# Weighted values as 64x64 squares of the array, interleaved with the scores, with no copies of the values

## The chip, the cores and the metric

The kernel runs on one core of one Trainium2 chip. The metric is the device time of one execution in microseconds (us); lower is better. Three runs of the kernel before took 3058.30, 3062.69 and 3063.12 us.

## What is computed

The input is 8 sequences of 1024 tokens with 128 features. The network is a sandwich: half of a two-layer local-attention block, then a global attention, then half of the same local block again.

```python
x = x + 0.5 * ffn(layernorm(x))      # two layers of local attention + gated MLP
x = x + attn(layernorm(x))           # one global attention, 1024 x 1024 per sequence
x = x + 0.5 * ffn(layernorm(x))      # the same two layers again
```

The change lies in the local attention (8 heads of 64 features, windows of 64 tokens). Of each layer this part matters:

```python
q, k, v = split(shift_token(x) @ wqkv)             # 512 columns each
q, k = rotary(l2norm(q) * q_scale), rotary(l2norm(k) * k_scale)
# window w of 64 queries sees the keys of windows w-1 and w (w = 0: its own only)
sim = q_w @ concat(k_{w-1}, k_w).T                 # 64 x 128 for each head
sim = where((i < j) | (i > j + 64), -inf, sim)     # i: query, j: key
o_w = softmax(sim) @ concat(v_{w-1}, v_w)          # 64 x 64 for each head
x = x + o @ wo
```

## The kernel before, in words

Everything is float32, apart from the mask, which is bf16. The 8192 tokens are 64 tiles of 128 tokens (8 tiles make a sequence; `m` is the tile's place in it, 0 to 7; `row` its place among the 64; `n` counts tiles over all layers). There are `LAYERS` = 4 local layers, so 256 tiles are worked on in all. A tile holds two windows: its queries 0 to 63 see keys 64 to 127 of the tile before and its own keys 0 to 63; its queries 64 to 127 see its own 128 keys.

Each engine has its own program, written out by hand as functions that are called slot by slot; semaphores tie them together. `program` runs, for each layer, `local_slot(L, s)` for s = 0 to 65, then `mlp_slot` for the 15 remaining groups of the MLP; the global attention runs between layers 1 and 2. Slot s of a local layer is a software pipeline: TensorE works on the scores of tile s, the weighted values of tile s - 1, the output projection of tile s - 2, the projections of tiles s + 3 and s + 4 and the transposes of q and k of tile s + 2. The order on TensorE in an ordinary slot (s from 1 to 59) is:

1. `scores(s)`: 4 bf16 matmuls write the mask into banks 3 and 4 of PSUM (L1184), then 16 float32 matmuls in 64x64 squares of the array add q @ k.T on top (L1194 for queries 0 to 63, L1196 for queries 64 to 127). Head 2*hh + i uses array rows 64*i to 64*i + 63 and bank 3 + i; the window of queries picks the array's columns. A float32 matmul appears in the profile as two passes, so there are 16 + 16 passes of L1194 and L1196 for a tile.
2. `weigh_values(s - 1)`: 16 matmuls with 128 rows (all keys of a window) and 64 columns (the queries), 65 elements long (64 features and a column of ones that gives the softmax's sum); L1238 for queries 64 to 127 from `v`, L1241 for queries 0 to 63 from `vprev`. Heads 0 to 3 go to bank 7, heads 4 to 7 to bank 2. Two passes each: 16 + 16.
3. `heads_transpose(s - 2)` (L1226), the q or k projection (L1264), the v projection (L1285), the other q or k projection (L1264), `project_out(s - 2)` (L1296), `weights_transpose(s, 0)` and `(s, 1)` (L1316), `keys_transpose` (L1330), `queries_transpose` (L1346).

In the last slots of a layer (s from 60 to 63, the branch `NT - 4 <= s < NT`) no q and k are projected any more, and `weights_transpose(s, 0)` comes right after `heads_transpose` and at most a v projection.

`vprev` is a second copy of the values, turned by half a tile, so that the 128 keys of the first window lie on partitions 0 to 127: SyncE's queue makes it with two DMAs for each tile (L437, L439), after waiting for ScalarE's copy of v (L594). `weigh_values` waits for them, and so does ScalarE before it writes v's next tile but two.

The other engines: VectorE takes the maxima of the scores (L789, both halves wait for `scores_ready`, which the last scores matmul raises), the reciprocal of the sums (L797, waits for `pv_ready`), the division (L804), the rotary products (L775, L780), sums of squares (L835) and the scaled q and k (L813). ScalarE takes the exponents (L566, after the maxima), squares (L573), and the copies out of PSUM: v (L594), oT (L587), probsT (L600), kT (L609, L610), qT (L612). In an ordinary slot ScalarE copies oT before the exponents; in the last slots it takes exponents 0 first. GpSimd takes the root (L491) and the sum q*cos + q*sin (L496); in layers 0 and 2 it also normalises two tiles in every second slot (L508 to L516). In each layer slot 64 (s == NT) has only the weighted values of the last tile.

The keys of a tile lie in `kT[rows, m % 4, head pair, 0:192]`: before, columns 0 to 63 hold the last 64 keys of the tile before and columns 64 to 191 the tile's own.

Of the kernel before, what the change touches and what calls it, by code (L numbers as in the profile page):

```python
# [13 lines left out]
P = 128  # L14
# [13 lines left out]
KT = WIN + P  # L28
VU = P + 3
# [22 lines left out]
def window_masks():  # L52

    i = np.arange(P)[:, None] % WIN
    j = np.arange(P)[None, :]
    open_ = (j >= i) & (j <= i + WIN)
    first = open_ & (j >= WIN)
    return np.stack([np.tile(np.where(m, 0.0, MASKED), (1, 4)) for m in (first, open_)]).astype(np.float32)  # L60
# [32 lines left out]
def before(t, k, times=1):  # L93


    return times * (t.n + 1 - k)
# [14 lines left out]
def macaron(nc, x_in, wq_in, bq_in, wk_in, bk_in, wv_att_in, bv_in, wo_att_in, bo_in,  # L111
# [15 lines left out]
    with ExitStack() as ctx:  # L127
# [10 lines left out]
        def bank(i, lo=0, hi=BANK, rows=slice(0, P)):  # L138
# [16 lines left out]
        mask = sb("mask", [P, 2, BANK], BF16)  # L155
# [13 lines left out]
        v = sb("v", [P, 4, HEADS, HD1])  # L169
        vprev = sb("vprev", [P, 4, HEADS, HD1])  # L170
# [22 lines left out]
        mask32 = probs.rearrange("p (t c) -> p t c", t=2)  # L193
# [12 lines left out]
        early = vprev[:].rearrange("p a b c -> p (a b c)")  # L206
# [18 lines left out]
         pv_ready, rsum_ready, o_ready, oT_psum, oT_ready, attn_ready, x1_ready,  # L225
# [6 lines left out]
         pv_ready rsum_ready o_ready oT_psum oT_ready attn_ready x1_ready stats_ready  # L232
# [9 lines left out]
        vprev_ready = [sem(f"vprev_ready{i}") for i in range(4)]  # L242
# [6 lines left out]
        def tile_at(L, row):  # L249
            return Tile(L, row, L * NT + row, row % MT) if 0 <= row < NT else None  # L250
# [87 lines left out]
        def _(sp):  # L338
# [91 lines left out]
            def local_slot(L, s):  # L430
                if t := late_tile(L, s + 6):
                    store_blocks(t)
                if t := late_tile(L, s + 5):
                    load_blocks(t)
                if t := tile_at(L, s + 3):
                    wait(sp, v_ready, before(t, 0))
                    sp.dma_start(vprev[WIN:P, t.m % 4], v[0:WIN, t.m % 4]).then_inc(vprev_ready[t.m % 4], 16)  # L437
                    lo = v[WIN:P, (t.m - 1) % 4] if t.m else v[0:WIN, 0]
                    sp.dma_start(vprev[0:WIN, t.m % 4], lo).then_inc(vprev_ready[t.m % 4], 16)  # L439
                if s == 2:  # L440
                    load_output(L)
                if s in (NT - 16, NT - 12, NT - 8):
                    load_tokens(L, (s - NT + 16) // 4)
# [115 lines left out]
        def _(act):  # L559
# [547 lines left out]
        def _(pe):  # L1107
# [62 lines left out]
            def scores(t):  # L1170

                wait(pe, qT_ready, before(t, 0))
                wait(pe, kT_ready, before(t, 0, 2))
                wait(pe, x1_ready, before(t, 3))
                wait(pe, probs_ready, before(t, 1, 2))
                if t.row == 0 and t.L == DEPTH:
                    pe.wait_ge(theta_ready, NT)
                    pe.wait_ge(pT_ready, 2 * NT)
                elif t.row == 0:
                    wait(pe, hid_ready, 3 * NG * t.L)  # L1180
                for w in range(2):
                    for i in range(2):
                        rows, queries = slice(WIN * i, WIN * i + WIN), slice(WIN * w, WIN * w + WIN)
                        nc.tensor.matmul(bank(3 + i, rows=queries), windows16[rows, queries],  # L1184
                                         mask[rows, 0 if w == 0 and t.m == 0 else 1, :],
                                         start=True, stop=False, skip_group_check=True)
# [42 lines left out]
            def weigh_values(t):  # L1229

                pe.wait_ge(vprev_ready[t.m % 4], 32 * (t.n // 4 + 1))
                wait(pe, o_ready, before(t, 1, 2))
                pe.wait_ge(probsT_ready, 2 * t.n + 2)
                for h in range(HEADS):
                    at_h = (h % 2) * BANK + (h // 2) * P
                    col = (h % 4) * HD1
                    bk = (7, 2)[h // 4]
                    nc.tensor.matmul(bank(bk, col, col + HD1, slice(WIN, P)),  # L1238
                                     probsT[:, at_h + WIN:at_h + P], v[:, t.m % 4, h, :],
                                     start=True, stop=True)  # L1240
                    last = nc.tensor.matmul(bank(bk, col, col + HD1, slice(0, WIN)),  # L1241
                                            probsT[:, at_h:at_h + WIN], vprev[:, t.m % 4, h, :],
                                            start=True, stop=True)
                last.then_inc(pv_ready, 1)
# [105 lines left out]
            def local_slot(L, s):  # L1350
# [11 lines left out]
                elif s == 0:  # L1362
# [6 lines left out]
                    scores(tile(0))  # L1369
# [7 lines left out]
                elif NT - 4 <= s < NT:  # L1377
                    scores(tile(0))
                    weigh_values(tile(-1))
# [13 lines left out]
                elif s < NT:  # L1393
                    scores(tile(0))
                    weigh_values(tile(-1))
# [15 lines left out]
                elif s == NT:  # L1411
                    weigh_values(tile(-1))
# [157 lines left out]
```

## Time and profile before

| | us |
|---|---|
| three runs: lowest, median, highest | 3058.30, 3062.69, 3063.12 |
| the profiled execution: its own time | 3062.09 |
| its span in the profile | 3060.3 |
| busy: TensorE (PE) | 2986.1 |
| busy: VectorE (DVE) | 2588.4 |
| busy: ScalarE (ACT) | 2093.9 |
| busy: GpSimd (POOL) | 1748.7 |

How to read it: the durations of matmuls are modelled and neighbouring matmuls overlap, so the busy time of TensorE says that it is hardly ever without work, and not how fast it goes. How fast it goes is read from the distance between the starts of its instructions. PEld is the loading of TensorE's weights, which overlaps the matmuls; its operand is the one that is kept in the array.

### The profile page before, as it was taken

How to read it: one execution, taken by the hardware profiler on the slowest of the kernel's cores; microseconds unless marked ns; L12 is line 12 of the kernel's file. 1: busy time of each engine (PE TensorE's matmuls, PEld its weight loads, DVE VectorE, ACT ScalarE, POOL GpSimd, SP SyncE). 2: the span in 40 equal slices, each digit the busy share in tenths (PEclk: the TensorE clock that was granted, in tenths of full speed). 3: DMA queues.
4: the chain of work that ended last, by engine and by line, in shares of the span. 5: the costliest groups of instructions: out<-in, count | busy, mean ns of one | idle time of the engine just before them, and what ended most of it. 6: DMA issues, size and time to landing. Idle time of an engine off the chain costs nothing.

```text
span 3060.3 us, 84552 instructions
## 1 busy us (share of the span) xinstructions
PE 2986.1 (98%) x30773; PEld 2157.1 (70%) x30773; DVE 2588.4 (85%) x5526; ACT 2093.9 (68%) x5016; POOL 1748.7 (57%) x1158
## 2 busy tenths in 40 slices
PE   7999999999999999989999799999999999999999
PEld 4777777667777777656777577777766677777765
DVE  7999998668888888858999699999866788888866
ACT  4777777436777777328889477777753677777742
POOL 8888886125666665541000688888721566666610
PEclk9999999999999999999999899999999999999999
DMA  5222222102222232100000122222320122222221
GB/s 131 50 50 52 51 57 63 45 18 48 51 49 52 50 64 60 41 1 1 1 1 1 24 52 52 51 51 56 65 52 14 43 50 52 50 52 58 57 49 42
DMA packets 311515, 138.26 MB, mean 45 GB/s; under 512 B 225897, under 2 KB 276546, under 8 KB 311106
## 3 DMA queue, kind: packets, MB, share of 16 engines
q1 hardware_dynamic: 311106, 132.84, 19.9%
q8 instruction: 252, 4.13, 0.6%
q14 instruction: 157, 1.29, 0.1%
HBM read 28.13 MB, written 19.66 MB: 16 GB/s over the span
## 4 chain that ended last, share of the span: by engine, by line
PE 90%; DVE 4%; issue 2%; POOL 2%; ACT 1%; SPq 0%; DMA 0%; DVEq 0%; ACTq 0%; POOLq 0%
PE psum L1264 14%; PE psum L1139 11%; PE psum L1238 8%; PE psum L1285 7%; PE psum L1296 7%; PE psum L1316 7%; PE psum L1194 6%; PE psum L1165 5%; PE psum L1226 5%; PE psum L1330 3%; PE psum L1346 3%; PE psum L1529 3%; PE psum L1505 3%; PE psum L1184 3%; PE psum L1515 2%
## 5 line engine op out<-in xcount | busy, mean ns | idle before, releaser
L491 POOL TENSOR_TENSOR rnorm<-ssq_floor,neg_half 128x16 f32<-128x16 f32 x256 | 750.7, 2932 | 491.0 <-DVE qkr L813 486.2
L566 ACT ACTIVATE shared<-psum,neg_max 128x128 f32<-128x128 f32 x2048 | 596.6, 397 | 39.8 <-DVE neg_max L789 39.8
L496 POOL TENSOR_TENSOR qk_cos<-qk_cos,qk_sin 128x1024 f32<-128x1024 f32 x256 | 607.3, 2372 | 0.0
L1264 PE MATMUL psum<-wqkv,hT 128*128 128x512 f32 x1024 | 532.2, 603 | 17.7 <-DVE qk_sin L775 9.5
L587 ACT COPY shared<-psum 128x512 f32<-128x512 f32 x256 | 150.3, 587 | 435.0 <-PE psum L1226 435.0
L775 DVE TENSOR_TENSOR qk_sin<-psum,sin 128x512 f32<-128x512 f32 x512 | 350.5, 685 | 97.9 <-ACT sq L573 96.6
L780 DVE TENSOR_TENSOR qk_cos<-psum,cos 128x512 f32<-128x512 f32 x512 | 350.6, 685 | 78.6 <-ACT sq L573 78.4
L625 ACT ACTIVATE shared<-psum,b1g 128x512 f32<-128x512 f32 (+1 forms) x192 | 131.7, 686 | 355.2 <-PE psum L1139 352.0
L1139 PE MATMUL psum<-shared,w1g 128*128 128x512 f32 (+1 forms) x768 | 347.2, 595 | 5.4 <-DVE shared L879 4.0
L573 ACT ACTIVATE sq<-psum 128x512 f32<-128x512 f32 x512 | 334.6, 654 | 25.2 <-PE psum L1264 25.2
L1296 PEld LDWEIGHTS psum<-wo,shared 128*128 128x128 f32 x2048 | 267.5, 191 | 115.7 <-issue 115.0
L789 DVE TENSOR_REDUCE neg_max<-psum 128x4 f32<-128x512 f32 x512 | 321.2, 666 | 23.6 <-PE psum L1196 23.4
L835 DVE TENSOR_REDUCE ssq<-sq 128x16 f32<-128x1024 f32 x256 | 309.4, 1209 | 0.6 <-POOL ssq_floor L488 0.6
L813 DVE TENSOR_TENSOR qkr<-qk_cos,rnorm 128x1024 f32<-128x1024 f32 x256 | 303.8, 1187 | 6.9 <-issue 6.3
L1238 PE MATMUL psum<-v,shared 128*64 128x65 f32 x4096 | 293.6, 224 | 0.0
L1241 PE MATMUL psum<-vprev,shared 128*64 128x65 f32 x4096 | 293.4, 224 | 0.0
L1238 PEld LDWEIGHTS psum<-v,shared 128*64 128x64 f32 x4096 | 258.1, 137 | 46.4 <-issue 46.4
L600 ACT COPY shared<-psum 128x512 f32<-128x512 f32 x512 | 285.3, 621 | 5.9 <-PE psum L1316 5.9
L1264 PEld LDWEIGHTS psum<-wqkv,hT 128*128 128x128 f32 x1024 | 177.3, 193 | 150.6 <-issue 139.3
L1285 PE MATMUL psum<-wqkv,hT 128*128 128x512 f32 x512 | 281.5, 632 | 0.0
L1316 PE MATMUL psum<-ident,shared 128*128 128x128 f32 x2048 | 270.7, 273 | 8.8 <-ACT shared L566 4.0
L1296 PE MATMUL psum<-wo,shared 128*128 128x128 f32 x2048 | 270.9, 275 | 0.0
(132 smaller groups left out, 6382.5 us busy)
## 6 DMA issues: line engine op xcount, KB each, us to landing
vprev<-v SPq DMA_DIRECT2D x512, 130.0 KB, 2.3
token_blocks<-blocks SPq DMA_DIRECT2D x236, 64.0 KB, 1.6
hT<-token_blocks SPq DMA_DIRECT2D x944, 16.0 KB, 1.8
shared<-Y SPq DMA_DIRECT2D x32, 256.0 KB
shared<-Y SPq DMA_DIRECT2D x32, 224.0 KB
out<-X SPq DMA_DIRECT2D x8, 512.0 KB, 3.2
X<-in_L_attn_x SPq DMA_DIRECT2D x7, 512.0 KB, 6.5
wqkv<-in_L_ffn_wqkv SPq DMA_DIRECT2D x4, 512.0 KB, 3.9
```

What stands on the lines that cost most here:

```text
L491: nc.gpsimd.tensor_tensor(rnorm[:], ssq_floor[:], neg_half[:], ALU.pow).then_inc(rnorm_ready, 1)
L496: nc.gpsimd.tensor_tensor(both, both, qk_sin[:, t.m % 2, :], ALU.add).then_inc(sum_ready, 1)
L566: last = nc.scalar.activation(probs[:, c * P:(c + 1) * P], bank(3 + i, (c % 4) * P, (c % 4 + 1) * P), ACT.Exp, bias=neg_max[:, c:c + 1])
L573: nc.scalar.activation(sq[:, i * INNER:(i + 1) * INNER], bank(i), ACT.Square).then_inc(sq_ready, 1)
L775: nc.vector.tensor_tensor(y, x[:, :, ::-1, :], part.unsqueeze(1).to_broadcast([P, HEADS, 2, DH // 2]), ALU.mult).then_inc(rot_ready, 1)
L780: nc.vector.tensor_tensor(heads(qk_cos[:, t.m % 2, i * INNER:(i + 1) * INNER]), heads(bank(i)), cos[:, t.m, i:i + 1, :].to_broadcast([P, H ...
L1139: last = nc.tensor.matmul(bank(banks[half], rows=slice(0, size)), w1g[:, half * HID + lo:half * HID + lo + size], zT, start=True, stop=True)
L1238: nc.tensor.matmul(bank(bk, col, col + HD1, slice(WIN, P)), probsT[:, at_h + WIN:at_h + P], v[:, t.m % 4, h, :], start=True, stop=True)
L1264: nc.tensor.matmul(bank(i), hT[:, t.m * P:(t.m + 1) * P], wqkv[:, i * INNER:(i + 1) * INNER], start=True, stop=True).then_inc(qk_psum, 1)
L1285: nc.tensor.matmul(bank(v_bank(t)), hT[:, t.m * P:(t.m + 1) * P], wqkv[:, 2 * INNER:3 * INNER], start=True, stop=True).then_inc(v_psum, 1)
L1296: last = nc.tensor.matmul(bank(out_bank(t), 0, P), oT[:, c * P:(c + 1) * P], wo[:, c, :], start=(c == 0), stop=(c == INNER // P - 1))
L1316: last = nc.tensor.transpose(bank(6 + i, (c % 4) * P, (c % 4 + 1) * P), probs[:, c * P:(c + 1) * P], ident[:])
```

## The change

The weighted values are computed in 64x64 squares, like the scores: for each head and window of queries, the own and the other 64 keys are two matmuls that add up in PSUM. Each has 64 rows, 64 columns and 65 elements, so a tile has 32 matmuls (64 passes) in place of 16 (32 passes); a first tile of a sequence (m = 0) has 28. They are made in two parts. In part 0 the array's upper rows work on heads 0 to 3 (bank 7) and its lower rows on heads 4 to 7 (bank 2); in part 1 it is the other way round and the sums are completed. Part 1 waits for a new semaphore, `pv_begun`, that part 0's last matmul raises. The scores are cut in two halves too (head pairs 0 and 1, then 2 and 3), and the order is scores half 0 (with the mask), values part 0, scores half 1, values part 1. In slot 0 the two halves of the scores follow each other, in slot 64 the two parts of the values do.

The keys of the tile now lie first in `kT` (columns 0 to 127), and those of the tile before in columns 128 to 191, so that a window's own keys have the same partitions in `probsT` as in `v`. For queries 0 to 63 the scores' moving operand is two pieces of 64 columns, 128 apart. The mask has three variants (768 KB in float32 instead of 512 KB), turned to fit.

`vprev`, its 512 DMAs, its semaphores and all waits for them are gone; `v` has five buffers instead of four, and the weights of the global attention, which lay in `vprev`'s space, have a tensor `early` of their own.

```diff
@@ sync: local_slot
-                if t := tile_at(L, s + 3):
-                    wait(sp, v_ready, before(t, 0))
-                    sp.dma_start(vprev[WIN:P, t.m % 4], v[0:WIN, t.m % 4]).then_inc(vprev_ready[t.m % 4], 16)
-                    lo = v[WIN:P, (t.m - 1) % 4] if t.m else v[0:WIN, 0]
-                    sp.dma_start(vprev[0:WIN, t.m % 4], lo).then_inc(vprev_ready[t.m % 4], 16)
@@ scalar: values, rotated
-                if u := tile_at(t.L, t.row - 3):
-                    act.wait_ge(vprev_ready[u.m % 4], 32 * (u.n // 4 + 1))
-                nc.scalar.copy(v[:, t.m % 4, :, 0:DH], heads(bank(v_bank(t)))).then_inc(v_ready, 1)
+                nc.scalar.copy(v[:, t.n % VALUES_KEPT, :, 0:DH], heads(bank(v_bank(t)))).then_inc(v_ready, 1)
...
-                nc.scalar.copy(kT[:, (t.m + 1) % 4, :, 0:WIN], src[:, :, WIN:P]).then_inc(kT_ready, 1)
-                nc.scalar.copy(kT[:, t.m % 4, :, WIN:KT], src).then_inc(kT_ready, 1)
+                nc.scalar.copy(kT[:, (t.m + 1) % 4, :, P:KT], src[:, :, WIN:P]).then_inc(kT_ready, 1)
+                nc.scalar.copy(kT[:, t.m % 4, :, 0:P], src).then_inc(kT_ready, 1)
@@ tensor: scores(t, second): waits and mask only if not second
-                lo = 0 if t.m else WIN
-                for hh in range(4):
+                blocks_of = 2 if t.m else 1
+                for hh in (2, 3) if second else (0, 1):
                     for i in range(2):
                         rows = slice(DH * i, DH * i + DH)
                         q = qT[rows, t.m % 2, hh, :]
                         k = kT[rows, t.m % 4, hh, :]
-                        nc.tensor.matmul(bank(3 + i, hh * P + lo, (hh + 1) * P, slice(0, WIN)), q[:, 0:WIN],
-                                         k[:, lo:P], start=False, stop=True, skip_group_check=True)
+                        own_then_before = k.rearrange("p (b j) -> p b j", j=WIN)[:, 0:2 * blocks_of - 1:2, :]
+                        to = bank(3 + i, hh * P, hh * P + blocks_of * WIN, slice(0, WIN)).rearrange("p (b j) -> p b j", j=WIN)
+                        nc.tensor.matmul(to, q[:, 0:WIN], own_then_before, start=False, stop=True, skip_group_check=True)
                         last = nc.tensor.matmul(bank(3 + i, hh * P, (hh + 1) * P, slice(WIN, P)), q[:, WIN:P],
-                                                k[:, WIN:KT], start=False, stop=True, skip_group_check=True)
-                last.then_inc(scores_ready, 1)
+                                                k[:, 0:P], start=False, stop=True, skip_group_check=True)
+                if second:
+                    last.then_inc(scores_ready, 1)
@@ tensor: weigh_values
-                pe.wait_ge(vprev_ready[t.m % 4], 32 * (t.n // 4 + 1))
-                wait(pe, o_ready, before(t, 1, 2))
-                pe.wait_ge(probsT_ready, 2 * t.n + 2)
-                for h in range(HEADS):
-                    at_h = (h % 2) * BANK + (h // 2) * P
-                    col = (h % 4) * HD1
-                    bk = (7, 2)[h // 4]
-                    nc.tensor.matmul(bank(bk, col, col + HD1, slice(WIN, P)),
-                                     probsT[:, at_h + WIN:at_h + P], v[:, t.m % 4, h, :], start=True, stop=True)
-                    last = nc.tensor.matmul(bank(bk, col, col + HD1, slice(0, WIN)),
-                                            probsT[:, at_h:at_h + WIN], vprev[:, t.m % 4, h, :], start=True, stop=True)
-                last.then_inc(pv_ready, 1)
+                if second:
+                    pe.wait_ge(pv_begun, t.n + 1)
+                else:
+                    wait(pe, v_ready, before(t, 0))
+                    wait(pe, o_ready, before(t, 1, 2))
+                    pe.wait_ge(probsT_ready, 2 * t.n + 2)
+                for j in range(HEADS // 2):
+                    for i in range(2):
+                        h = j + HEADS // 2 * (second ^ i)
+                        at_h = (h % 2) * BANK + (h // 2) * P
+                        col = (h % 4) * HD1
+                        rows = slice(WIN * i, WIN * i + WIN)
+                        for w in range(2):
+                            alone = w == 0 and t.m == 0
+                            if alone and i == 1:
+                                continue
+                            n = t.n - 1 if i > w else t.n
+                            last = nc.tensor.matmul(bank((7, 2)[h // 4], col, col + HD1, slice(WIN * w, WIN * w + WIN)),
+                                                    probsT[rows, at_h + WIN * w:at_h + WIN * w + WIN],
+                                                    v[rows, n % VALUES_KEPT, h, :], start=j == 0 and (alone or not second),
+                                                    stop=alone or bool(second), skip_group_check=True)
+                last.then_inc(pv_ready if second else pv_begun, 1)
@@ tensor: local_slot, both branches from s = 1 to NT - 1
-                    scores(tile(0))
-                    weigh_values(tile(-1))
+                    for second in range(2):
+                        scores(tile(0), second)
+                        weigh_values(tile(-1), second)
```

## Rows read from the trace of the kernel before

**Rows 1.** The page: busy time, granted clock in 40 slices, chain that ended last.
```profile
PE 2986.1 (98%) x30773; PEld 2157.1 (70%) x30773; DVE 2588.4 (85%) x5526; ACT 2093.9 (68%) x5016; POOL 1748.7 (57%) x1158
...
PEclk9999999999999999999999899999999999999999
...
PE 90%; DVE 4%; issue 2%; POOL 2%; ACT 1%; SPq 0%; DMA 0%; DVEq 0%; ACTq 0%; POOLq 0%
```

**Rows 2.** PE timeline, an ordinary slot: start us, length us, line, count.
```profile
311.93 0.41 PE L1184 MATMUL psum<-mask,windows 64*64 64x512 bf16 x4
312.17 0.27 PE L1194 MATMUL psum<-kT,qT 64*64 64x128 f32 x2
312.17 0.27 PE L1196 MATMUL psum<-kT,qT 64*64 64x128 f32 x2
312.27 0.27 PE L1194 MATMUL psum<-kT,qT 64*64 64x128 f32 x2
...
312.94 0.27 PE L1196 MATMUL psum<-kT,qT 64*64 64x128 f32 x2
313.14 0.27 PE L1238 MATMUL psum<-v,shared 128*64 128x65 f32 x1
...
313.25 0.22 PE L1238 MATMUL psum<-v,shared 128*64 128x65 f32 x1
...
314.07 0.22 PE L1238 MATMUL psum<-v,shared 128*64 128x65 f32 x1
...
314.22 0.66 PE L1226 MATMUL psum<-ident,shared 128*128 128x128 f32 x4
...
320.11 0.41 PE L1184 MATMUL psum<-mask,windows 64*64 64x512 bf16 x4
```

**Rows 3.** PE timeline, a sequence's first tile: its L1194 has 64 columns.
```profile
303.99 0.22 PE L1194 MATMUL psum<-kT,qT 64*64 64x64 f32 x2
303.99 0.27 PE L1196 MATMUL psum<-kT,qT 64*64 64x128 f32 x2
304.04 0.28 PE L1194 MATMUL psum<-kT,qT 64*64 64x64 f32 x3
```

**Rows 4.** PEld timeline: weight loads right after PE had waited.
```profile
41.62 0.13 PEld L1184 LDWEIGHTS psum<-mask,windows 64*64 64x64 bf16 x4 [1.50 <-issue]
41.65 0.20 PEld L1194 LDWEIGHTS psum<-kT,qT 64*64 64x64 f32 x2
```

**Rows 5.** ACT timeline, the slots of rows 2: copies of oT and probsT.
```profile
314.92 0.59 ACT L587 COPY shared<-psum 128x512 f32<-128x512 f32 x1 [1.84 <-PE psum L1226]
...
318.90 1.11 ACT L600 COPY shared<-psum 128x512 f32<-128x512 f32 x2
```

**Rows 6.** DVE timeline, the slot that begins at 320.11.
```profile
321.64 1.25 DVE L789 TENSOR_REDUCE neg_max<-psum 128x4 f32<-128x512 f32 x2
...
325.25 0.69 DVE L775 TENSOR_TENSOR qk_sin<-psum,sin 128x512 f32<-128x512 f32 x1 [0.43 <-ACT sq L573]
```

**Rows 7.** POOL timeline, a sum and the next tile's root.
```profile
312.58 2.37 POOL L496 TENSOR_TENSOR qk_cos<-qk_cos,qk_sin 128x1024 f32<-128x1024 f32 x1
...
316.72 2.93 POOL L491 TENSOR_TENSOR rnorm<-ssq_floor,neg_half 128x16 f32<-128x16 f32 x1 [1.55 <-DVE qkr L813]
```

**Rows 8.** Timelines of DVE, ACT and PE in slot 61 of layer 0.
```profile
540.53 1.29 DVE L789 TENSOR_REDUCE neg_max<-psum 128x4 f32<-128x512 f32 x2 [2.27 <-PE psum L1196]
...
541.26 1.14 ACT L566 ACTIVATE shared<-psum,neg_max 128x128 f32<-128x128 f32 x4 [1.01 <-DVE neg_max L789]
...
542.45 0.66 PE L1316 MATMUL psum<-ident,shared 128*128 128x128 f32 x4 [0.33 <-ACT shared L566]
```

**Rows 9.** DVE timeline, an early slot of layer 2.
```profile
1757.12 1.23 DVE L813 TENSOR_TENSOR qkr<-qk_cos,rnorm 128x1024 f32<-128x1024 f32 x1 [0.95 <-issue]
```

**Rows 10.** DMA issues of the whole span: count, KB each, us to landing.
```profile
vprev<-v SPq DMA_DIRECT2D x512, 130.0 KB, 2.3
```

**Rows 11.** The tile `mask`: ns min/median/max, when, form.
```profile
L948 DVE CAST mask<-shared x1: 683/683/683, 29.2 to 29.2; 128x1024 bf16<-128x1024 f32 x1
```

More of the change, by code:

```diff
@@ L59, in window_masks @@
     first = open_ & (j >= WIN)
-    return np.stack([np.tile(np.where(m, 0.0, MASKED), (1, 4)) for m in (first, open_)]).astype(np.float32)
+    turned = [np.roll(m, WIN, axis=1) for m in (first, open_)]
+    return np.stack([np.tile(np.where(m, 0.0, MASKED), (1, 4)) for m in turned + [open_]]).astype(np.float32)
 class Tile:
@@ L154, in macaron @@
         sin = sb("sin", [P, MT, 2, DH])
-        mask = sb("mask", [P, 2, BANK], BF16)
+        mask = sb("mask", [P, 3, BANK], BF16)
         windows16 = sb("windows16", [P, P], BF16)
@@ L168, in macaron @@
         kT = sb("kT", [P, 4, 4, KT])
-        v = sb("v", [P, 4, HEADS, HD1])
-        vprev = sb("vprev", [P, 4, HEADS, HD1])
+        v = sb("v", [P, VALUES_KEPT, HEADS, HD1])
+        early = sb("early", [P, 10 * P + 3])
         neg_max = sb("neg_max", [P, HEADS])
@@ L1168, in combine, with scores @@
                 last.then_inc(mlp_ready, 1)
[L1170 to L1186, printed above, removed]
-                lo = 0 if t.m else WIN
-                for hh in range(4):
+            def scores(t, second):
+                if not second:
+                    wait(pe, qT_ready, before(t, 0))
+                    wait(pe, kT_ready, before(t, 0, 2))
+                    wait(pe, x1_ready, before(t, 3))
+                    wait(pe, probs_ready, before(t, 1, 2))
+                    if t.row == 0 and t.L == DEPTH:
+                        pe.wait_ge(theta_ready, NT)
+                        pe.wait_ge(pT_ready, 2 * NT)
+                    elif t.row == 0:
+                        wait(pe, hid_ready, 3 * NG * t.L)
+                    for w in range(2):
+                        for i in range(2):
+                            rows, queries = slice(WIN * i, WIN * i + WIN), slice(WIN * w, WIN * w + WIN)
+                            nc.tensor.matmul(bank(3 + i, rows=queries), windows16[rows, queries],
+                                             mask[rows, 2 if w else 1 if t.m else 0, :],
+                                             start=True, stop=False, skip_group_check=True)
+                blocks_of = 2 if t.m else 1
+                for hh in (2, 3) if second else (0, 1):
                     for i in range(2):
@@ L1227, in heads_transpose, with weigh_values @@
                 last.then_inc(oT_psum, 1)
-            def weigh_values(t):
-                pe.wait_ge(vprev_ready[t.m % 4], 32 * (t.n // 4 + 1))
-                wait(pe, o_ready, before(t, 1, 2))
-                pe.wait_ge(probsT_ready, 2 * t.n + 2)
-                for h in range(HEADS):
-                    at_h = (h % 2) * BANK + (h // 2) * P
-                    col = (h % 4) * HD1
-                    bk = (7, 2)[h // 4]
-                    nc.tensor.matmul(bank(bk, col, col + HD1, slice(WIN, P)),
-                                     probsT[:, at_h + WIN:at_h + P], v[:, t.m % 4, h, :],
-                                     start=True, stop=True)
-                    last = nc.tensor.matmul(bank(bk, col, col + HD1, slice(0, WIN)),
-                                            probsT[:, at_h:at_h + WIN], vprev[:, t.m % 4, h, :],
-                                            start=True, stop=True)
-                last.then_inc(pv_ready, 1)
+            def weigh_values(t, second):
+                if second:
[5 more added lines that the diff above has]
+                for j in range(HEADS // 2):
+                    for i in range(2):
+                        h = j + HEADS // 2 * (second ^ i)
+                        at_h = (h % 2) * BANK + (h // 2) * P
+                        col = (h % 4) * HD1
+                        rows = slice(WIN * i, WIN * i + WIN)
+                        for w in range(2):
+                            alone = w == 0 and t.m == 0
[7 more added lines that the diff above has]
+                last.then_inc(pv_ready if second else pv_begun, 1)
             def project_qk(t, i):
@@ L1368, in local_slot @@
                         pe.wait_ge(consts_done, 9)
-                    scores(tile(0))
+                    scores(tile(0), 0)
+                    scores(tile(0), 1)
                     project_v(tile(3))
@@ L1393, in local_slot @@
                 elif s < NT:
-                    scores(tile(0))
-                    weigh_values(tile(-1))
+                    for second in range(2):
+                        scores(tile(0), second)
+                        weigh_values(tile(-1), second)
                     if t := tile(-2):
@@ L1411, in local_slot @@
                 elif s == NT:
-                    weigh_values(tile(-1))
+                    weigh_values(tile(-1), 0)
+                    weigh_values(tile(-1), 1)
                     heads_transpose(tile(-2))
```

10 lines of the change are left out of this document (4 added, 6 removed).

## The prediction, made before the change was run

> **What bounds the kernel.** I read the page first. TensorE is busy 98% of the span and carries 90% of the chain that ended last [rows 1]. The reader is to see that only what changes the distance between TensorE's starts changes the time, as long as VectorE (85%), the next engine, keeps up. So the second view is TensorE's timeline over an ordinary slot [rows 2]. Masks of two tiles that follow each other start at 311.93 and 320.11, so a slot takes 8.18 us, and this distance repeats unchanged from slot 4 to slot 59 of every layer. In such a slot TensorE waits for nobody. The third views are the timelines of ScalarE, VectorE and GpSimd in the same slots [rows 5 to 7], for the slack that each leaves, and of a layer's last slots [rows 8], where TensorE does wait.
>
> **The passes themselves: no gain.** A tile's values take 32 passes in two column halves of the array. L1238 starts at 313.14, 313.25 and for the sixteenth time at 314.07 [rows 2]: after the first distance of 0.11 the other 14 take 0.82, so 0.058 us each for 65 elements. Afterwards there are 64 passes in four squares, again 16 rounds. If four squares go side by side, a round costs what it costs now. For that, scores are the nearest rows: two L1194 and two L1196 start at 312.17 within the resolution of the row, the next L1194 at 312.27, and 8 rounds of four go from 312.17 to 312.94, 0.11 us each [rows 2]. A square whose scores have only 64 columns takes its next pass after 0.05 to 0.06 us (303.99 to 304.04) while the other two squares work [rows 3]. So both halves of the claim are seen, four at once and 0.058 for such a short pass, but not together. The dearest end is that passes can't follow faster than they do in scores, 0.11 / 4 = 0.027 us each: 64 x 0.027 = 1.74 us where the values' 0.93 us (313.14 to 314.07) and their two seams are now. The cheapest end is that nothing changes: 16 x 0.058 = 0.93. I take this end, as rows 3 stand nearer to it (two squares at 0.058 and two at 0.11 are 0.019 per pass, already beyond 0.027).
>
> **The seam between scores and values: the gain.** Scores use 64x64 squares, the values 128x64. From the last round of scores (312.94) to the first pass of values are 0.20 us where a round of scores takes 0.11, and from there to the second pass 0.11 where a pass takes 0.058 [rows 2]. Without a change of shape the two distances should be 0.11 and 0.058: the seam costs 0.31 - 0.17 = 0.14 us. It goes. The change from the values to the 128-row transposes (314.07 to 314.22) remains, as does the one ahead of the mask, so nothing else is saved. The new order has three seams, all within one shape. The trace has one of this kind, mask to scores: 0.24 us (311.93 to 312.17 [rows 2]) for 512 bf16 columns, which at TensorE's full clock of 2.4 GHz, granted nearly throughout [rows 1], are 0.21. So a seam costs between nothing and 0.03 us. I take nothing, because in this one the operands change from bf16 to float32 too, and keep 0.03 for one seam of each slot (8 us) for the range.
>
> By the Trainium skill (TensorEngine Tiling (Array Packing), Key Properties) a change of tiling mode drains TensorE, and a change of tile alone doesn't. The 0.14 us at the seam agree [rows 2]; how much is drain and how much the first load, the rows don't tell.
>
> **Ordinary slots.** 8.18 - 0.14 = 8.04 us. They are 56 in each layer (4 to 59), 224 in all. Slots 1 to 3 of layers 1 and 3 show no wait that binds either: 6 more. 230 x 0.14 = 32.2 us saved. In slots 1 to 3 of layers 0 and 2 GpSimd's sum is late (VectorE stands 0.95 us before L813 [rows 9]) and TensorE waits behind it; there I count no gain.
>
> Does another engine stop 8.04 us? The moved step is the second half of the scores: `scores_ready` now comes 8 rounds of 0.058, 0.47 us, after where it did. Behind it stand VectorE's maxima, and behind them on its queue the sums, L813, L804 and L775. Counted from the mask at 320.11, the last scores end at 320.11 + 1.01 + 0.27 = 321.39 and would end at 321.86; VectorE starts the maxima at 321.64, so they come 0.2 us later, and in this slot VectorE has 0.43 us idle before L775 [rows 6], which takes it up. In the slot before, VectorE is busy with statistics until after the new time. GpSimd's loop in layers 0 and 2: the root waits for L813, and over two slots this is the tightest loop. The sum ends at 314.95 and the root starts at 316.72, with L813's 1.18 us between [rows 7]; the remaining 0.59, less some 0.2 for passing on, leaves 0.4 of slack over two slots, and 0.28 are taken from them. It fits, narrowly. ScalarE has 1.84 us idle before L587 [rows 5].
>
> The new order wants probsT earlier: the values start 0.24 + 4 x 0.11 = 0.68 after the mask, not 1.21. ScalarE's copy ends at 318.90 + 1.11 = 320.01 [rows 5], the values would start at 320.79. Fulfilled.
>
> **The new wait, `pv_begun`.** Part 1 waits until part 0's last matmul is done; queued behind it on TensorE is all else. Let T be the start of part 0's last pass. It is done at T + 0.22; passing on costs 0.04 (L1226 ends at 314.88, L587 starts at 314.92 [rows 2, 5]) and taking up 0.05 (L566 ends at 542.40, L1316 starts at 542.45 [rows 8]): T + 0.31. Scores half 1 fills T + 0.06 to T + 0.49. So its cover has 0.18 us to spare. After a wait, six loads start within 0.03 us, four of the mask and two of the scores [rows 4], so the queue fills quickly. Where the cover is missing, in slot 64, the wait costs 0.31 - 0.06 = 0.25: 4 layers, 1.0 us. If the cover failed wholly in the other slots, they would lose 0.25 instead of nothing.
>
> **The last slots: a loss.** In slots 61 to 63 the chain is scores, maxima (starts 540.53 right after L1196), exponents (541.26), and TensorE waits 0.33 us for these with L1316 [rows 8]. With `scores_ready` 0.47 later, each of these slots becomes 0.47 longer instead of 0.14 shorter. In slot 60 TensorE doesn't wait yet, but by the same chain would now by some 0.2, less 0.14: 0.05. Sum 3 x 0.47 + 0.05 = 1.45, in 4 layers 5.8 us.
>
> **DMAs and the rest.** 512 DMAs of 130 KB go, 2.3 us each to landing [rows 10]. No wait of TensorE ends on one, and SyncE's queue loses two waits ahead of the token blocks, which aren't late: nothing gained, at the cheapest end 1 us from slots in which tokens come early. The mask's load grows by half and its cast from 0.68 to 1.0 us [rows 11]; it stands in VectorE's queue at the start, where TensorE waits for VectorE: 0.5 us, at most 1.3 with the longer transfer. ScalarE's copies have the same sizes. The scores' moving operand in two pieces costs nothing or at most the difference of two 64-column passes to one of 128, 2 x 0.058 - 0.11 = 0.007 in 8 rounds, 0.06 us a tile, 14 us in all; I take nothing, since nothing is read twice.
>
> **Sum.** -32.2 + 5.8 + 1.0 + 0.5 = -24.9 us. The profiled execution took 3062.1 us (its span 3060.3); 3037.2. The median of the runs is 0.6 above it: 3038 us. A change by less than 0.2% (6 us) can't be told from none here.
>
> **Rivals.** *A, the squares don't keep the pace (slower).* Place: the passes of `weigh_values`. It decides from (0.93 + 0.14) / 64 = 0.0167 us per pass on; four squares at the round of 0.058 are 0.0145, the fastest the trace shows is 0.019 [rows 3]. At 0.019 a tile loses 0.15 net, over 256 tiles +38, and 3108 us with the last slots; at 0.027 a tile loses 0.67 net, +172 and some 3240. Against it: six loads within 0.03 us [rows 4], and four scores passes that start together [rows 2]. Chance 0.15.
>
> The Trainium skill (TensorE: Matmul & The Clock Gate, Wait — 56ns, not 53.3ns?) states that start-to-start never falls below about 25 ns for a small matmul; this is nearly the case of 0.027 above. Estimated from that page, 64 x 25 ns = 1.6 us, +0.53 a tile, some 3205 us. This case's trace disagrees for different squares (four passes start together) and leaves the average open.
>
> *B, the wait shows.* Completion of a pass in a square may be told later than I take. Each 0.1 us of lateness beyond 0.18 costs 0.1 a slot; at 0.1 exposed (0.28 late) the gain of 25 is gone, with 0.25 exposed the time is 3095. Chance 0.07.
>
> *C, another engine takes over.* VectorE with GpSimd in layers 0 and 2, or the last slots lose more: half of the ordinary gain, 3038 + 16 = 3054. For it: 0.4 of slack against 0.28. Chance 0.08.
>
> Forecast: 0.70, with its own range of 3024 (passes at 0.056, 8 us; slots 1 to 3 of layers 0 and 2 gain too, 1 us; the last slots lose nothing, 5.8) to 3052 (the operand in two pieces or the seams and half of the former). B below 0.1 exposed and C still are faster. Range of 8 in 10: 3022 to 3075, which takes in C and the milder half of B, and leaves out A (0.15). Faster 0.77, same 0.07 (B near its deciding point, the edge of C), slower 0.16.
>
> **What would show it.** Masks in ordinary slots 8.04 apart; the first pass of values 0.11 after the last scores round of half 0, with four squares each 0.058; no stand of TensorE ahead of part 1 except in slot 64; L1316 of the last slots waiting about 0.8 instead of 0.33; no L1330 wait for VectorE in ordinary slots. Wrong would make it: rounds of values over 0.067 us, a gap of over 0.1 after scores half 1, or VectorE's L813 standing for GpSimd in every second slot.

## The result

The changed kernel takes 3045.61 us (median of 4 runs, 3039.54 to 3046.97), the kernel before 3062.52 us (4 runs, 3058.3 to 3063.12). The ratio is 0.9944, its 95% interval 0.9931 to 0.9958: 0.56% faster, 17 us where 25 were forecast. The profiled execution has a span of 3044.0 us, 16.3 less than before.

First the page of the changed kernel: TensorE's busy time and passes, and the DMA queues (packets, MB, share of 16 engines).

```profile
PE 2956.9 (97%) x38453; PEld 2167.1 (71%) x38453; DVE 2601.1 (85%) x5526; ACT 2090.6 (69%) x5016; POOL 1751.8 (58%) x1158
...
q1 hardware_dynamic: 270274, 64.91, 9.8%
q8 instruction: 312, 5.11, 0.7%
```

TensorE has 7680 passes more (38453 against 30773 [rows 1]): 256 x 32 more for the values, less 512 that the first tiles of the sequences leave out. (Such a tile has 24 matmuls of values, not 28 as the section on the change says.) For the doubled passes of the values the time went down, so squares do overlap. The instruction queue moves 312 packets of 16 KB; it moved 252 before: 60 more for 2 x 7680 = 15360 more instructions of TensorE (a load and a matmul for each pass), so one packet for each 256.

Next TensorE's timeline of the changed kernel in an ordinary slot (start us, length us, line, count), the counterpart of [rows 2].

```profile
317.62 0.41 PE L1178 MATMUL psum<-mask,windows 64*64 64x512 bf16 x4
317.86 0.27 PE L1190 MATMUL psum<-kT,qT 64*64 64x128 f32 x2
...
318.19 0.27 PE L1191 MATMUL psum<-kT,qT 64*64 64x128 f32 x2
318.30 0.64 PE L1244 MATMUL psum<-v,shared 64*64 64x65 f32 x32
318.76 0.27 PE L1190 MATMUL psum<-kT,qT 64*64 64x128 f32 x2
...
319.09 0.27 PE L1190 MATMUL psum<-kT,qT 64*64 64x128 f32 x2
...
319.20 0.64 PE L1244 MATMUL psum<-v,shared 64*64 64x65 f32 x32
319.77 0.44 PE L1222 MATMUL psum<-ident,shared 128*128 128x128 f32 x2
```

The first values start 0.11 after the last round of scores (318.19 to 318.30): the 0.20 of before is gone. The 32 passes of part 0 take 318.30 to 318.76, 8 rounds of 0.0575. Scores half 1 follows without a gap, and so does part 1 at 319.20. Next the view by stages, over the whole slot: its length, busy us of PE, PEld, DVE, ACT and POOL with the number of instructions, granted clock, DMA share, GB/s.

```profile
317.62:325.65 8.03, 8.03 (x135) 6.12 (x135) 7.37 (x15) 6.33 (x18) 7.59 (x7) 1.00 0.09 18
```

8.03 us where 8.18 were. That is the slot of the prediction, 8.04. But not all ordinary slots look so. Reading the starts of the masks (L1178) through the trace, 199 of the 224 ordinary slots take 8.03 us within 0.03 and the other 25 take 0.15 to 1.07 more, 9.4 us in all; before, no ordinary slot differed from 8.18. This is slot 4 of layer 0, again TensorE's timeline.

```profile
74.87 0.41 PE L1178 MATMUL psum<-mask,windows 64*64 64x512 bf16 x4
...
76.45 0.63 PE L1244 MATMUL psum<-v,shared 64*64 64x65 f32 x26
77.81 0.34 PE L1244 MATMUL psum<-v,shared 64*64 64x65 f32 x6 [0.74 <-issue]
...
83.97 0.41 PE L1178 MATMUL psum<-mask,windows 64*64 64x512 bf16 x4
```

The slot takes 9.10 us. After 26 of the 32 passes of part 1 TensorE stands, and the cause is "issue": no semaphore that the profile knows. Of the 25 stands 20 are inside the values, 4 right behind them (ahead of L1222) and one behind the transposes that follow (ahead of L1268). This was in no step of the prediction.

The last slots of a layer, the counterpart of [rows 8]: TensorE and VectorE in slot 61 of layer 0, and then TensorE's rows of the same slot before that [rows 8] doesn't have.

```profile
533.57 0.41 PE L1178 MATMUL psum<-mask,windows 64*64 64x512 bf16 x4
535.71 0.66 PE L1222 MATMUL psum<-ident,shared 128*128 128x128 f32 x4
537.32 0.66 PE L1320 MATMUL psum<-ident,shared 128*128 128x128 f32 x4 [0.95 <-ACT shared L561]
537.81 1.14 PE L1300 MATMUL psum<-wo,shared 128*128 128x128 f32 x8
538.83 0.66 PE L1320 MATMUL psum<-ident,shared 128*128 128x128 f32 x4
...
540.29 0.41 PE L1178 MATMUL psum<-mask,windows 64*64 64x512 bf16 x4
```
```profile
535.39 1.29 DVE L782 TENSOR_REDUCE neg_max<-psum 128x4 f32<-128x512 f32 x2 [2.84 <-PE psum L1191]
```
```profile
539.17 0.41 PE L1184 MATMUL psum<-mask,windows 64*64 64x512 bf16 x4
...
541.47 0.66 PE L1226 MATMUL psum<-ident,shared 128*128 128x128 f32 x4
542.45 0.66 PE L1316 MATMUL psum<-ident,shared 128*128 128x128 f32 x4 [0.33 <-ACT shared L566]
542.94 1.14 PE L1296 MATMUL psum<-wo,shared 128*128 128x128 f32 x8
544.24 0.63 PE L1316 MATMUL psum<-ident,shared 128*128 128x128 f32 x4
```

Slot 61 takes 6.72 us instead of 6.50. TensorE waits 0.95 us for the exponents instead of 0.33, since the maxima start 1.82 us after the mask (535.39 less 533.57) instead of 1.36 (540.53 less 539.17). L1320 starts 3.75 us after the mask, where L1316 started 3.28 after it: 0.47 later, as forecast. Its second group starts only 0.19 later (5.26 instead of 5.07), because before TensorE also lost time between L1296 and that group (1.30 us from start to start, now 1.02). So the slot grows by 0.22 and not by 0.47.

So the account of the span, from the masks' starts in the two traces, is:

| stretch | forecast | measured |
|---|---|---|
| ordinary slots, 224 x (8.18 to 8.03) | -31.4 | -33.6 |
| stands inside the values | 0 | +9.4 |
| slots 0 to 3 of the four layers | -0.8 | +0.5 |
| slots 60 to 62, four layers | +4.0 | +3.3 |
| slots 63 and 64 and what follows | +2.9 | +3.9 |
| before the first mask | +0.5 | +0.3 |
| sum (of the unrounded terms) | -24.9 | -16.2 |

One trace is not the median of the runs. The fifth row holds the stretch from slot 63 of layer 1 over the global attention, which takes 518.4 to 525.2 us in the nine traces; in this trace it is 1.5 us longer than before, in the second trace of the same kernel (below) 0.9 shorter. The other three layers lose 0.79 us each in both. In that second trace the sum is -18.0, with stands of 9.5 us.

### The profile page after: what moved, and what is told of

It reads as the page before. It is cut to its first block, busy times and chain, and to the rows that moved or that the text cites. A ratio compares the mean times of both kernels' runs of the same rounds, so it can differ in the third digit from the quotient of the medians.

```text
span 3044.0 us, 99399 instructions
## 1 busy us (share of the span) xinstructions
PE 2956.9 (97%) x38453; PEld 2167.1 (71%) x38453; DVE 2601.1 (85%) x5526; ACT 2090.6 (69%) x5016; POOL 1751.8 (58%) x1158
## 4 chain that ended last, share of the span: by engine, by line
PE 91%; DVE 3%; POOL 2%; issue 2%; ACT 1%; SPq 0%; DMA 0%; DVEq 0%; ACTq 0%; POOLq 0%
PE psum L1268 14%; PE psum L1132 11%; PE psum L1244 8%; PE psum L1300 7%; PE psum L1289 7%; PE psum L1320 7%; PE psum L1190 6%; PE psum L1158 5%; PE psum L1222 5%; PE psum L1334 4%; PE psum L1350 3%; PE psum L1537 3%; PE psum L1513 3%; PE psum L1178 3%; PE psum L1523 2%
## 5 line engine op out<-in xcount | busy, mean ns | idle before, releaser
L1268 PE MATMUL psum<-wqkv,hT 128*128 128x512 f32 x1024 | 534.5, 606 | 19.2 <-DVE qk_sin L768 10.3
L782 DVE TENSOR_REDUCE neg_max<-psum 128x4 f32<-128x512 f32 x512 | 328.0, 682 | 73.9 <-PE psum L1191 73.8
L1244 PE MATMUL psum<-v,shared 64*64 64x65 f32 x15872 | 342.1, 218 | 3.7 <-issue 3.0
L1244 PEld LDWEIGHTS psum<-v,shared 64*64 64x64 f32 x15872 | 317.9, 134 | 9.1 <-issue 7.5
L1191 PE MATMUL psum<-kT,qT 64*64 64x128 f32 x4096 | 308.0, 270 | 0.0
L1190 PE MATMUL psum<-kT,qT 64*64 64x128 f32 (+1 forms) x4096 | 301.3, 264 | 0.0
L1268 PEld LDWEIGHTS psum<-wqkv,hT 128*128 128x128 f32 x1024 | 178.2, 194 | 153.5 <-issue 141.7
L1320 PE MATMUL psum<-ident,shared 128*128 128x128 f32 x2048 | 271.5, 274 | 14.8 <-ACT shared L561 11.6
```

The source lines that it names most:

```text
L1190: nc.tensor.matmul(to, q[:, 0:WIN], own_then_before, start=False, stop=True, skip_group_check=True)
L1244: last = nc.tensor.matmul(bank((7, 2)[h // 4], col, col + HD1, slice(WIN * w, WIN * w + WIN)), probsT[rows, at_h + WIN * w:at_h + WIN * w ...
L1268: nc.tensor.matmul(bank(i), hT[:, t.m * P:(t.m + 1) * P], wqkv[:, i * INNER:(i + 1) * INNER], start=True, stop=True).then_inc(qk_psum, 1)
L1320: last = nc.tensor.transpose(bank(6 + i, (c % 4) * P, (c % 4 + 1) * P), probs[:, c * P:(c + 1) * P], ident[:])
```

## The experiments

All runs below are measured against the kernel before on their chip, 3062.2 to 3062.7 us. Theory F: the stands come where TensorE's queue runs dry because a block of its instructions is fetched too late for the dense stretch of squares. Theory T: they come from something that runs beside the kernel in time.

**The changed kernel again.**

> The changed kernel once more, for the comparison on one chip and for a second trace. In its first trace TensorE stands without a wait (cause 'issue') inside part 1 of the values in some 20 of the 224 ordinary slots, by 0.2 to 1.07 us, 9.4 us in all; in layer 0 in slots 4, 5, 18, 31, 32 and 46. Theory F (these stands are TensorE's queue running dry where a block of its instructions has to be fetched, so their place goes with the count of instructions): the same slots of layer 0 again, within one; 3037 to 3049 us. Theory T (they come from something that runs in time beside the kernel): other slots.

3046.91 us (5 runs, 3044.11 to 3049.79), ratio 0.9951 (0.9938 to 0.9963). In its trace the stands of layer 0 are in slots 4, 5, 18, 19, 31, 32 and 46, and 9.5 us in all: the same places within one slot, with other lengths. In the other layers the places come back too, apart from slot 42 of layer 2 (0.56 us in the first trace).

**128 instructions ahead of everything.**

```diff
@@ tensor: ahead of program
             pe.wait_ge(consts_done, 4)
+            for _ in range(32):
+                nc.tensor.matmul(bank(7, 0, 1), ident[:], ident[:, 0:1], start=True, stop=True)
             program(local_slot, mlp_slot, global_slot)
```

> The changed kernel with 32 one-column matmuls (128 instructions of TensorE: 64 passes with their weight loads) ahead of everything, into a bank that nobody reads; it adds work that the reference doesn't need. A slot has 278 instructions of TensorE, 246 where the values are those of a sequence's first tile, 274 on average, 18 more than 256. Theory F with blocks of 256 instructions (the instruction queue moves packets of 16 KB): 128 instructions more put the stands of layer 0 some 128 / 18 = 7 slots away from 4, 5, 18, 31, 32, 46, so near 11, 25, 38 or 39, 53. Theory T: no such shift; the same slots, or any.

3049.6 us (one run), 9.9 us of stands. Its first mask starts at 50.53 us instead of 41.91, behind the added matmuls, so its time isn't to be compared with the others. In layer 0 they are now in slots 11, 12, 24, 38, 40, 53 and 54, where theory F put 11, 25, 38 or 39, and 53. Slots 4, 5, 18, 31, 32 and 46 take 8.03 us. This is slot 24 of layer 0, on TensorE's timeline; two passes of part 1 come late.

```profile
244.29 0.41 PE L1178 MATMUL psum<-mask,windows 64*64 64x512 bf16 x4
...
245.79 0.70 PE L1244 MATMUL psum<-v,shared 64*64 64x65 f32 x28
...
247.18 0.27 PE L1244 MATMUL psum<-v,shared 64*64 64x65 f32 x2 [0.68 <-issue]
```

So a stand belongs to a place in the sequence of TensorE's instructions, with a period of 256 of them. Theory T has fallen.

The traces allow a closer look, as they hold each packet of the instruction queue with its start and duration, and every instruction of TensorE, semaphore instructions included. Counted from the first of these as 0, all 25 stands of the changed kernel's first trace come at place 193 to 195 of a block of 256, and so they do in the second trace and, with 128 instructions more ahead, here. With packets and blocks paired in order, TensorE goes on 1.2 to 1.6 us after the end of the packet that came last, in all 25; no block's place 193 is reached earlier than 1.2 us after its packet's end. In the kernel before the nearest is 4.6 us. Theory F holds: at a stand TensorE waits for a block of its instructions. Of what the 1.2 us consist, no run shows.

**The copies kept.** The changed kernel, and two DMAs of the values for each tile behind the old waits, now to DRAM.

```diff
@@ sync: local_slot
+                if t := tile_at(L, s + 3):
+                    wait(sp, v_ready, before(t, 0))
+                    wait(sp, vprev_ready[0], 32 * t.n)
+                    sp.dma_start(vprev[t.n % 2, WIN:P], v[0:WIN, t.n % VALUES_KEPT]).then_inc(vprev_ready[0], 16)
+                    lo = v[WIN:P, (t.n - 1) % VALUES_KEPT] if t.m else v[0:WIN, t.n % VALUES_KEPT]
+                    sp.dma_start(vprev[t.n % 2, 0:WIN], lo).then_inc(vprev_ready[0], 16)
@@ scalar: values
+                if u := tile_at(t.L, t.row - 3):
+                    act.wait_ge(vprev_ready[0], 32 * (u.n + 1))
```

> The changed kernel, but SyncE still issues two DMAs of the values for each tile behind the same waits (to DRAM, where nobody reads them), and ScalarE waits for them before it writes v as before. If the transfers were hidden in the kernel before, as predicted, the time is that of the changed kernel, within 2 us. Rival, their removal brought part of the gain (token blocks earlier, less traffic): 5 to 15 us more.

3055.39 us (10 runs, 3051.12 to 3060.07), ratio 0.998 (0.9971 to 0.999): 8.5 us slower than the changed kernel's 3046.91 on another chip (the intervals of the two ratios don't overlap), so the rival had the number right. But the place isn't the token blocks. An ordinary slot without a stand still takes 8.03 us; the stands have grown from 9.4 to 20.5 us, at much the same places. One of the longest, slot 35 of layer 1 (9.36 us), first the timeline, then the loads' idle time by cause in this kernel, and the same in the changed kernel.

```profile
987.58 0.41 PE L1188 MATMUL psum<-mask,windows 64*64 64x512 bf16 x4
...
989.16 0.62 PE L1254 MATMUL psum<-v,shared 64*64 64x65 f32 x26
990.79 0.34 PE L1254 MATMUL psum<-v,shared 64*64 64x65 f32 x6 [1.00 <-issue]
...
996.94 0.41 PE L1188 MATMUL psum<-mask,windows 64*64 64x512 bf16 x4
```
```profile
  issue: 24.0, 41
```
```profile
  issue: 10.5, 22
```

The second and third of these are the view of one source line: the idle us and the times before the values' passes and loads (L1254 here, L1244 there). With the copies' traffic the same blocks come later: the packet of this slot starts 0.35 us after the mask and takes 1.34, in the changed kernel it starts 0.19 ahead of the mask and takes 1.12. So it ends 0.76 later, and the stand has grown from 0.51 to 1.33. The kernel before had this traffic and no stands: from a mask to the transposes behind the values it has 68 passes in 2.3 us, where the changed kernel has 100 in 2.15. The spans of the two traces differ by 6.4 us only, since the stretch with the global attention is 4.1 us shorter in this one; the price of 8.5 is that of the medians.

**All slots in sequence.** Both halves of the scores, then both parts of the values.

```diff
@@ tensor: local_slot, both branches from s = 1 to NT - 1
-                    for second in range(2):
-                        scores(tile(0), second)
-                        weigh_values(tile(-1), second)
+                    for second in range(2):
+                        scores(tile(0), second)
+                    for second in range(2):
+                        weigh_values(tile(-1), second)
```

> In all slots both halves of the scores come first, then both parts of the values; the cover of the wait for pv_begun is gone. By the prediction's sum 0.25 us is exposed in each ordinary slot: 8.03 + 0.25 = 8.28, and 3041 + 56 = 3097 us, slower than the kernel before by some 35 us. Rival, order among squares is kept by the array anyway and the wait costs nothing: 8.03 and 3041. Stands inside the values (theory F) stay.

3105.97 us (4 runs), ratio 1.0146 (1.0133 to 1.016). Ordinary slots take 8.36 us, so the bare wait costs up to 0.33, not 0.25. The profile names it, before the weight loads of the values (idle us, times):

```profile
  PE psum L1244: 59.7, 256
```

In the changed kernel this line reads 0.9 us, 4 times: only in slot 64, where the parts follow each other. Read pass by pass, the last pass of part 0 starts at 319.17 in one such slot and the first of part 1 at 319.46, in the changed kernel's slot 64 at 554.63 and 554.93: 0.30 us, which is the 0.31 of the prediction and 0.25 more than a round. The round behind it takes 0.108 instead of 0.058; that is the part that the prediction's 0.25 lacks. Scores half 1 covers 0.49 (318.71 to 319.20 in the changed kernel), so the cover holds with 0.18 to spare, as forecast. The stands shrink to 3.0 us in 10 slots, against my remark that they stay. It fits that the pause in the middle of the values leaves time for the next block.

**The old values, interleaved.** The kernel before; scores and values (128x64, with vprev) cut in halves and interleaved as in the changed kernel, with no wait between.

```diff
@@ tensor: weigh_values (waits only if not second, pv_ready only if second; scores likewise)
-                for h in range(HEADS):
+                for h in range(4 * second, 4 * second + 4):
@@ local_slot
-                    scores(tile(0))
-                    weigh_values(tile(-1))
+                    for second in range(2):
+                        scores(tile(0), second)
+                        weigh_values(tile(-1), second)
```

> The kernel before, its values still 128x64 with vprev, but scores and values cut in halves and interleaved (heads 0 to 3, then 4 to 7; no wait between). Three changes between 64x64 and 128x64 in each slot instead of one. If a change of the array's shape is the price of the seam, 0.14 us each, two more are +0.28 in a slot, +65 us over 230 slots, and with the later maxima in the last slots some 3135 us. Rival, the seam of before is paid for the three semaphore waits ahead of the values, not for the shape: no waits stand at the new seams, 3065 to 3072 us with the last slots' loss.

3144.08 us (4 runs), ratio 1.0266 (1.0251 to 1.0282). The time is 9 us over the expected 3135. All ordinary slots take 8.49 us, 0.31 more than 8.18 for two more changes of shape: 0.155 each. No semaphore wait stands at the seam back to the scores or at the one after it, so the shape is what costs, and not the semaphores. TensorE's timeline at the seam from values to scores:

```profile
304.44 0.22 PE L1241 MATMUL psum<-v,shared 128*64 128x65 f32 x1
...
304.50 0.22 PE L1241 MATMUL psum<-v,shared 128*64 128x65 f32 x1
...
304.65 0.32 PE L1195 MATMUL psum<-kT,qT 64*64 64x128 f32 x1
...
304.81 0.27 PE L1195 MATMUL psum<-kT,qT 64*64 64x128 f32 x1
...
304.92 0.27 PE L1195 MATMUL psum<-kT,qT 64*64 64x128 f32 x1
```

0.15 us to the first round of scores (304.50 to 304.65) where 0.058 is the rhythm, and 0.16 to the second (304.81) where 0.11 is. This kernel has no stand in any ordinary slot; place 193 of a block is never reached earlier than 5.5 us after the end of its packet.

**The last slots in sequence.** Only slots 60 to 63 get the sequential order, by the diff of the kernel with all slots in sequence.

> In slots 60 to 63 both halves of the scores come first, then both parts of the values. If the loss of the last slots is the later scores_ready, as predicted, the maxima come 0.47 us earlier and the wait for pv_begun (0.25) is paid in its place, part of it under the wait for the exponents: slots 60 to 62 take 6.49, 6.50 and 6.03 us where they take 6.72, 6.72 and 6.29 now, and with slot 63 4 us less in all than the changed kernel: 3041. Rival, the last slots are longer for another reason (the squares themselves): no gain, or 1 us per layer more by the wait.

3041.09 us (5 runs, 3038.65 to 3042.61), ratio 0.9932 (0.992 to 0.9944), 5.8 us less than the changed kernel on the same chip; no run of one is within the range of the other. Slots 60 to 62 take 6.56, 6.38 and 6.19 us. TensorE's timeline in slot 61, to be compared with the one above:

```profile
533.58 0.41 PE L1178 MATMUL psum<-mask,windows 64*64 64x512 bf16 x4
534.69 1.43 PE L1244 MATMUL psum<-v,shared 64*64 64x65 f32 x64
536.05 0.66 PE L1222 MATMUL psum<-ident,shared 128*128 128x128 f32 x4
536.86 0.66 PE L1320 MATMUL psum<-ident,shared 128*128 128x128 f32 x4
...
539.96 0.41 PE L1178 MATMUL psum<-mask,windows 64*64 64x512 bf16 x4
```

The values end later (L1222 2.47 us after the mask instead of 2.14), but L1320 starts 3.28 us after the mask instead of 3.75. So the later `scores_ready` is the loss: of the 0.82 us per layer over slots 60 to 62, 0.60 come back, and 0.22 stay. From slot 60 to the next layer the masks gain 1.0 us per layer, 4.1 in all; the rest of the 5.8 is within the scatter of the two kernels.

**Both ends in sequence.** Slots 1 to 3 as well.

> Slots 1 to 3 and 60 to 63 in sequence (both halves of the scores, then both parts of the values), all others as in the changed kernel. In slot 1 of layers 1 and 3 the changed kernel takes 7.39 us and the fully sequential one 6.97; slots 2 and 3 of layers 0 and 2 are the same in both; slots 2 and 3 of layers 1 and 3 are 0.10 and 0.33 longer in sequence. So layers 1 and 3 are even (-0.42 + 0.10 + 0.33), and the time is that of the kernel with only its last slots in sequence: 3041, within 2 us. The stands inside the values stay, about 9 us in all. Rival: stands come and go with the place of the blocks, up to 3 us either way.

3042.64 us (5 runs, 3038.44 to 3045.07), ratio 0.9931 (0.9917 to 0.9945), the same as the last slots alone. Slot 1 of layers 1 and 3 falls from 7.39 to 6.97 us, slots 2 and 3 rise from 8.26 and 8.03 to 8.36, and stands are 10.9 us in this trace.

## Why the prediction was right, and where it was off

**Passes four at a time.** Right. Part 0 takes 8 rounds of 0.0575 (the slot at 317.62); rival A, passes that don't keep the pace, has fallen as a rule of the array. The Trainium skill (TensorE: Matmul & The Clock Gate, Wait — 56ns, not 53.3ns?) gives a floor of some 25 ns from start to start; here 32 passes to different squares take 0.46 us, 14.4 ns each, so the measurement decides against it for passes in different squares. What supplies the passes is another matter, below.

**The seam.** Right: forecast 0.14 us, 0.15 in the changed kernel, 0.155 where two were added. The new seams within one shape cost nothing.

**The new wait.** Right that it is covered, and right in the 0.31 us from a pass's start to the first pass behind the wait (0.30 measured) and in the reserve of 0.18. Its bare price was up to 0.33, not 0.25: the sum left out that the round behind a wait takes 0.05 us more. In slot 64, where the wait stands bare, that is 0.2 us over four layers; most of the 1 us by which slots 63 and 64 with what follows came out dearer is the scatter of the global attention.

**The last slots.** Right in cause and nearly in size: 0.82 us per layer over slots 60 to 62 where 0.99 was forecast. The single slots came otherwise: slot 60, with no wait before, lost 0.34 instead of 0.05, slots 61 and 62 0.22 and 0.26 instead of 0.47. The first L1320 is 0.47 late, as forecast; that 0.28 of it would come back ahead of the second one, where TensorE already lost time before, I hadn't seen. In slot 60 it is the second exponents that TensorE waits for (they end at 532.06, L1320 starts at 532.11), which the sum didn't have. The wait of L1320 came out as 0.95 us and not as some 0.8, since TensorE reaches it 0.16 earlier.

**Slots 1 to 3.** Off by a little: that no wait binds there was a wrong reading. Slot 1 of layers 1 and 3 became 0.47 us longer, not 0.14 shorter: the maxima are later there too, and TensorE waits 0.47 us for VectorE ahead of L1334. In sequence it takes 6.97 against 6.92 before.

**The step that failed: "DMAs and the rest", and the sum's silence on instructions.** The sum costed the supply of instructions at nothing; it took it for granted that TensorE's queue is always full. The rows that I read for it were six loads within 0.03 us after a wait [rows 4]; they show that a full queue empties quickly, not that a burst of 100 passes is supplied. The burst from the mask to the last value now holds 100 of the slot's 134 passes in 2.15 us; it held 68 in 2.3. Where place 193 of a block falls into its end, TensorE stands, 9.4 us in all. In the first trace that is all of the 8.7 us between forecast and measured sum, to within 1 us; in the second the stands are 9.5 us and the difference is 6.9. Shown are the place (the count of instructions), the packet (TensorE goes on 1.2 to 1.6 us after the end of the one for its block, at every stand), the dependence on the DMA traffic (20.5 us with the copies) and that a thinner burst has less (3.0) or none (the old values, interleaved). Open is why a packet isn't asked for earlier.

The transfers of the values, costed at nothing, were hidden in the kernel before, but not in the one after: kept, they would have taken back 8.5 us of its gain. Neither this term nor the stands had been priced; that the time still lies in the stated range is owed to the width of the range and not to these steps.

**Rivals B and C.** B (the wait shows) fell in the changed kernel. C (another engine takes over) fell: no wait of TensorE for VectorE or GpSimd stands in an ordinary slot; its number, 3054, was nearer than its mechanism.

## What to carry to other kernels

Squares of one shape next to each other are worth ordering for: each change of the array's shape cost 0.15 us here, and a dependency of TensorE on itself needs 0.3 us of other passes between, which another half of the scores gave. Before doubling the count of short passes, look at what supplies them: a dense stretch of TensorE instructions can run its queue dry though each pass would fit, and then DMA traffic that looked hidden has a price. Where a step is interleaved, ask for each stage of the loop who waits for its last half; in the last slots the plain order was better, and a kernel with both orders (3041 us) beats both kernels.

## What the runs showed of the hardware

- TensorE started 32 float32 passes with their own weights, each 64x64 with 65 columns, in 0.46 us: 14.4 ns per pass over four squares.
- The instruction queue moved one packet of 16 KB for each 256 instructions of TensorE (60 packets more for 15360 instructions more).
- Place 193 of a block (counted from 0) was never reached earlier than 1.2 us after the end of its packet. Where it fell into the end of a dense stretch (100 passes in 2.15 us), passes came late by 0.1 to 1.6 us a slot; 128 instructions at the start of the program moved these places by 7 slots, and 130 KB transfers beside it doubled the loss.
- A change between the 64x64 and the 128x64 shape cost 0.14 to 0.155 us.
- From the start of the last pass of a group to the first pass behind a wait of TensorE for it: 0.30 us. The round of passes after that took 0.108 us instead of 0.058.
